# A transformer block on one core: the written order of every engine's steps is set anew, and the inverse lengths get two buffers

## The reference, cut to what matters

```
x  = x + ga * trajectories(layernorm(x) * (1 + ca) + sa)     # "new": guidance mix over an 8-row window
y  = layernorm(x) * (1 + cb) + sb
for layer in (0, 1):
    q, k, v = split(shift_token(y) @ wqkv)                   # "proj": 8 heads of 64
    q, k = rotary(l2norm(q) * qs), rotary(l2norm(k) * ks)    # inverse lengths, then turning
    y = y + local_attention(q, k, v) @ wo                    # "a": windows of 64, each sees itself and the last
    h = layernorm(shift_token(y)) * lg + lb
    y = y + (a * gelu(g)) @ w2 + b2, with a, g = split(h @ w1 + b1)      # "ff"
out = x + gb * y
```

## Time and profile before

| | |
|---|---|
| median of three runs | 968.1 us (965.94 to 968.76) |
| the profiled execution, its own time | 966.96 us |
| its span, first to last instruction | 965.0 us |
| mean granted clock of PE | 0.942 of full |
| busy: PE, DVE, ACT, POOL | 786.4, 668.0, 659.3, 539.6 us |
| chain that ended last | PE 40%, DVE 20%, ACT 19%, "issue" 11%, POOL 9% |

### The profile page before, as it was taken

The page is one execution under the profiler, slowest core; times in us unless marked ns, Lnnn a source line. Parts: engine busy times, 40 slices in busy tenths (PEclk is TensorE's granted clock), DMA queues, the critical chain, the costliest instruction groups (busy, mean ns, idle before and its releaser), DMA issues.

```text
span 965.0 us, 19306 instructions
## 1 busy us (share of the span) xinstructions
PE 786.4 (81%) x7151; PEld 556.3 (58%) x7151; DVE 668.0 (69%) x1588; ACT 659.3 (68%) x1545; POOL 539.6 (56%) x324
## 2 busy tenths in 40 slices
...
DMA packets 12275, 9.85 MB, mean 10 GB/s; under 512 B 1040, under 2 KB 11288, under 8 KB 12184
## 3 DMA queue, kind: packets, MB, share of 16 engines
...
## 4 chain that ended last, share of the span: by engine, by line
PE 40%; DVE 20%; ACT 19%; issue 11%; POOL 9%; DMA 0%; SPq 0%; POOLq 0%; ACTq 0%; DVEq 0%
ACT probs L964 7%; PE pair L696 6%; PE mixed L727 5%; POOL qk L1494 4%; PE dense L831 4%; PE pair L759 3%; DVE space L1393 3%; DVE q_norm L1398 3%; PE dense L795 3%; PE dense L796 2%; PE dense L797 2%; DVE qk L1195 2%; PE dense L908 2%; ACT squares L1083 2%; ACT probs_t L972 2%
## 5 line engine op out<-in xcount | busy, mean ns | idle before, releaser
L1494 POOL TENSOR_TENSOR qk<-space 128x512 f32<-128x512 f32 x128 | 186.4, 1463 | 58.0 <-DVE q_norm L1398 55.1
L1454 POOL TENSOR_TENSOR root<-power,minus_half 128x32 f32<-128x32 f32 x32 | 174.0, 5438 | 4.6 <-DVE power L1404 4.6
L964 ACT ACTIVATE probs<-pair,neg_max 128x128 f32<-128x128 f32 x512 | 138.3, 402 | 18.9 <-DVE neg_max L1215 18.5
L1393 DVE TENSOR_TENSOR space<-dense,tables 128x512 f32<-128x512 f32 x128 | 87.5, 684 | 36.9 <-ACT space L1087 35.2
L908 PE MATMUL dense<-wq_hi,h_hi 128*128 128x512 f32 x192 | 90.2, 470 | 26.6 <-DVE space L1393 10.9
L1491 POOL TENSOR_TENSOR space<-space,tables 128x512 f32<-128x512 f32 x64 | 82.7, 1293 | 50.7 <-ACT space L1087 50.7
L696 PE MATMUL pair<-eye_s,probs 128*128 128x128 f32 x512 | 80.9, 292 | 34.9 <-ACT probs L964 34.7
L1215 DVE TENSOR_REDUCE neg_max<-pair 128x4 f32<-128x512 f32 x128 | 82.0, 684 | 35.2 <-PE pair L759 35.1
L1083 ACT ACTIVATE squares<-dense 128x512 f32<-128x512 f32 x128 | 79.1, 618 | 39.5 <-PE dense L910 38.6
L696 PEld LDWEIGHTS pair<-eye_s,probs 128*128 128x128 f32 x512 | 59.1, 146 | 56.2 <-ACT probs L964 51.9
L1398 DVE TENSOR_REDUCE q_norm<-squares 128x8 f32<-128x512 f32 x128 | 86.4, 675 | 0.0
...
## 6 DMA issues: line engine op xcount, KB each, us to landing
...
```

Source lines behind the costliest of these rows:

```text
L964: last = act.activation(probs[:, ring, hh, :], banks[m][:, hh * P:(hh + 1) * P], ACT.Exp, bias=neg_max[:, ring, hh:hh + 1], scale=1.0)
L1393: dve.tensor_tensor(turned_s[:, t % 2, m, :].rearrange("p (h a b) -> p h a b", h=HEADS, a=2), halves[:, :, ::-1, :], rot(layer, t, 2 * m + 1),
L1454: return pool.tensor_tensor(to, of, minus_half[:, 0:of.shape[-1]], ALU.pow)
L1494: pool.tensor_tensor(qk[s][:, t, m * INNER:(m + 1) * INNER], turned_c[:, t % 2, m, :], turned_s[:, t % 2, m, :], ALU.add).then_inc(added, 1)
```

## The change

Three things change, and no instruction is added or removed apart from waits.

1. `power` and `root` become `powers` and `roots` with two buffers each, used in turn by pair of tiles. `proj.rsqrt` on DVE additionally waits until the root of two pairs ago is written, and the root on POOL until the scaling of two pairs ago has been done.
2. All lists of `ORDER` except the lead-in are rewritten. Of 672 PE steps 338 stand at another place, of 592 on ACT 369, of 544 on DVE 262, of 240 on POOL 64, by at most 14 places.
3. With it the banks `dense`, which are dealt out in PE's order, fall to other steps.

```diff
-        power, root, scratch = sb("power", [P, 32]), sb("root", [P, 32]), sb("scratch", [P, 1])
+        powers, roots, scratch = sb("powers", [P, 2, 32]), sb("roots", [P, 2, 32]), sb("scratch", [P, 1])
...
-                dve.tensor_tensor(rows, rows, root[:, :].rearrange("p (h o) -> p h o", o=1)
+                dve.tensor_tensor(rows, rows, roots[:, pair_ % 2, :].rearrange("p (h o) -> p h o", o=1)
...
-                    dve.tensor_scalar(power[:, :], q_norm[:, :], 1e-24, None, ALU.max).then_inc(qk_powered, 1)
+                    if past(pair_ - 1):
+                        dve.wait_ge(qk_rooted, pair_ - 1)
+                    dve.tensor_scalar(powers[:, pair_ % 2, :], q_norm[:, :], 1e-24, None, ALU.max).then_inc(qk_powered, 1)
...
-                inverse_root(root[:, :], power[:, :]).then_inc(qk_rooted, 1)
+                if past(pair_ - 1):
+                    pool.wait_ge(qk_ready, pair_ - 1)
+                inverse_root(roots[:, pair_ % 2, :], powers[:, pair_ % 2, :]).then_inc(qk_rooted, 1)
```

The moves of which the text below speaks, as they stand in turn 1, unless said otherwise (`...` leaves out steps):

```diff
 PE, slot 1 to 2
-1:a.flip.2 1:proj.tile.1.1 1:proj.tile.1.2 1:a.mix.2 1:proj.tile.2.0 ... 1:a.flip.3 1:a.out.2 1:a.mix.3 1:proj.tile.3.0 1:proj.tile.3.1 1:proj.tile.3.2 1:a.out.3 2:new.dots 1:a.project 2:proj.tile.0.0 2:a.turn.0
+1:a.flip.2 1:proj.tile.1.1 1:proj.tile.1.2 1:proj.tile.2.0 1:a.mix.2 ... 1:proj.tile.3.0 1:a.flip.3 1:proj.tile.3.1 1:a.mix.3 1:proj.tile.3.2 1:a.out.2 2:new.dots 1:a.out.3 1:a.project 2:a.turn.0 2:a.turn.1 2:proj.tile.0.0
 PE, slot 0
-0:a.flip.2 0:proj.tile.0.0 0:proj.tile.0.1 0:proj.tile.0.2 0:a.mix.2 0:proj.tile.1.0 0:proj.tile.1.1 0:proj.tile.1.2 0:a.flip.3 0:proj.tile.2.0 ...
+0:a.flip.2 0:proj.tile.0.0 0:proj.tile.0.1 0:proj.tile.0.2 0:proj.tile.1.0 ... 0:proj.tile.2.2 0:a.flip.3 0:a.mix.2 0:a.mix.3 0:proj.tile.3.0 ...
 DVE, slot 1 to 2
-1:a.mix.2 1:proj.tile.2.0 1:proj.tile.2.1 1:a.mix.3 1:proj.tile.3.0 1:proj.unit.0 1:proj.tile.3.1 2:proj.split 1:proj.rsqrt.1 2:new.dots 1:a.project
+1:proj.tile.2.0 1:proj.tile.2.1 1:a.mix.2 1:proj.tile.3.0 1:proj.tile.3.1 1:a.mix.3 1:proj.rsqrt.1 2:proj.split 1:proj.unit.0 1:a.project
 DVE, slot 1, feed-forward
-1:ff.hi 1:a.mix.0 1:a.unit 1:a.mix.1 1:ff.up.0
+1:ff.hi 1:a.mix.0 1:ff.up.0 1:a.unit 1:ff.up.1 1:a.mix.1
 DVE, slot 1 to 2, turn 3
-1:a.mix.2 1:proj.tile.2.0 1:proj.tile.2.1 1:a.mix.3 1:proj.tile.3.0 1:proj.unit.0 1:proj.tile.3.1 2:proj.split
+1:proj.tile.2.0 1:proj.tile.2.1 1:a.mix.2 1:a.mix.3 1:proj.tile.3.0 1:proj.tile.3.1 2:proj.split 1:proj.unit.0
 DVE, slot 2
-2:new.gate 2:ff.hi 2:new.again
+2:ff.hi 2:new.gate 2:new.again
 POOL, slot 1 (turns 1 to 3)
-1:ff.stats 1:a.rsqrt 2:new.stats 1:ff.hi
+1:ff.stats 1:a.rsqrt 1:ff.hi 2:new.stats
 POOL, slot 1, turn 2
-1:proj.split 2:new.steps 1:proj.tile.0.0 ... 1:proj.rsqrt.0 1:proj.tile.2.0 ... 2:proj.split 1:proj.tile.3.1
+1:proj.split 1:proj.tile.0.0 ... 2:new.steps 1:proj.rsqrt.0 2:proj.split 1:proj.tile.2.0 ... 1:proj.tile.3.1
 ACT, slot 3, turn 2
-3:ff.norm 3:new.sims 3:a.out.2 ... 3:ff.up.0
+3:new.sims 3:a.out.2 3:ff.norm ... 3:ff.up.0
```

More of the change, by code:

```diff
@@ L65 @@
[L65 to L91, removed]
@@ L145 @@
+        2:a.mix.2 2:a.out.2 2:a.flip.3 2:ff.up.2 2:a.mix.3 2:ff.down 2:a.out.3 2:a.project 2:store.turn
+        3:ff.stats 3:ff.norm 3:ff.up.0 3:ff.up.1 3:ff.up.2 3:ff.down 3:store.turn"""),
     ],
@@ L280 @@
-        2:proj.tile.3.0 2:a.mix.3 2:proj.tile.3.1 2:new.gate 2:ff.hi 2:new.again 2:a.project 2:proj.rsqrt.1
-        2:new.stream 2:ff.up.0 2:ff.up.1 2:ff.up.2 3:a.unit 2:ff.down 3:proj.split 3:a.score.0 3:a.score.1
-        2:store.turn 2:proj.keep 3:proj.tile.0.0 3:proj.tile.0.1 3:a.mix.0 3:proj.tile.1.0 3:new.stats
-        3:proj.tile.1.1 3:new.turn 3:proj.rsqrt.0 3:proj.tile.2.0 3:proj.tile.2.1 3:a.mix.1 3:ff.stats
-        3:a.score.2 3:ff.norm 3:a.score.3 3:proj.unit.0 3:new.dots 3:a.mix.2 3:proj.tile.3.0 3:new.sims
@@ L312 @@
[L312 to L316 removed]
+        2:new.stats 2:new.turn 2:proj.split 2:proj.tile.0.0 2:proj.tile.0.1 2:proj.tile.1.0 2:proj.tile.1.1
@@ new lines @@
+        2:new.weights 2:a.mix.1 2:proj.tile.0.0 2:proj.tile.0.1 2:proj.tile.1.0 2:proj.tile.1.1
+        2:proj.rsqrt.0 2:proj.tile.2.0 2:proj.tile.2.1 2:a.score.2 2:a.score.3 2:ff.stats 2:ff.norm
+        2:a.mix.2 2:proj.unit.0 2:proj.tile.3.0 2:a.mix.3 2:proj.tile.3.1 2:ff.hi 2:new.gate 2:new.again
+        2:ff.up.0 2:new.stream 2:proj.rsqrt.1 2:ff.up.1 2:a.project 2:ff.up.2 3:a.unit 3:proj.split
+        2:ff.down 3:a.score.0 3:a.score.1 2:store.turn 2:proj.keep 3:proj.tile.0.0 3:proj.tile.0.1
```

497 lines of the change are left out of this document (262 added, 235 removed).

## The result

The changed kernel takes 982.96 us (median of 4 runs, 981.34 to 984.42) against 967.02 (965.27 to 968.76): ratio 1.0167, 95% interval 1.0149 to 1.0185, 16 us slower. The forecast was 953.0, and its range ended at 974. The profiled execution took 984.01 us, its span was 982.1 and PE's mean granted clock 0.946.

A forecast was written before the change was run, and what follows sets the result against it. No engine bounds the kernel as a whole; PE's 178.6 us of idle time is what an order can win from. Terms 5.7 + 3.6 + 1.5 + 1.3 + 3 = 15.1 us gave 968.1 - 15.1 = 953.0 us, range 935 to 974.

The forecast's parts named there:

- the rest of the order: Hundreds of swapped steps not priced singly, bounded by turn 2's list reaching turn 1's level: 3 us won, bounds 0 and 8.
- What bounds the kernel: No engine as a whole; 58 us stretches between projections are those where POOL is fullest, 41.2 us, the most anywhere.
- Two buffers: Second buffers for power and root: their added waits cost nothing, and by themselves they free nothing.
- `h_lo` ahead of `new.stats`: POOL, slot 1 of three turns: h_lo right behind the long root, 5.7 us won, bounds 0 and 6.0.
- The hand-over: Slot 1 to slot 2: bank for new.dots free earlier, projection at full clock; 3.6 us won, bounds 0 and 7.
- The clock at `ff.up`: PE, 214 to 221: shorter stop may keep the clock, granted 0.52 before; 1.5 us won, bounds 0 and 3.1.
- Table loads: ACT, turn 2: 3:new.sims ahead of 3:ff.norm saves two loads; 1.3 us won, bounds 0 and 2.6.
- Tiles ahead of attention: Rival: PE tiles waiting for banks delay attention, some 3 us in slots 0 and 1 of four turns; 977 us, chance 0.17.
- Nothing: Rival: waits removed come back at the next meeting of attention and POOL; about 968 us, chance 0.11.
- the 3 us priced there: POOL, turn 2: 2:proj.split ahead of 1:proj.tile.2.0 waits for the last product, a loss of some 3 us.
- The lock rule: Rival: long root blocks a DVE scaling, up to 5.4 us in each of three slots 1; 969 us, chance 0.02.

The follow-up runs named there:

- e4: Changed kernel with POOL's new.dots of slot 3 put back behind the additions of proj.tile.2.0 and 2.1, turns 1 and 2: 974.19 us, ratio 1.0083.
- e7: Kernel before with only POOL's new.dots of slot 3 moved ahead of proj.tile.2.0 and 2.1 additions, turns 1 and 2: 977.62 us, ratio 1.0098.
- e11: Kernel before plus two buffers, with only the late steps of 3|0 in the new order on PE, ACT and DVE: 970.14 us, ratio 1.0038.
- e1: Changed code with two buffers and their waits, but every list of the kernel before: 966.95 us, ratio 1.0005.
- e8: Kernel before plus two buffers, with only turn 1's hand-over from slot 1 to 2 in new order on PE, ACT, DVE: 970.41 us, ratio 1.0029.
- e3: Changed kernel with the new order only up to the projection of 1|1 and the order of before after it: 967.03 us, ratio 1.0002.
- e6: e4 with POOL's turn 2 list partly put back (new.steps ahead of slot 1's additions, proj.split behind tile 3.0's): 980.60 us, ratio 1.0126.
- e13: Kernel before plus two buffers, with the edits of e7 and e11 together: 979.24 us, ratio 1.0121.
- e5: e4 with the late steps of 3|0 also in the old order on PE, ACT and DVE: 974.10 us, ratio 1.0067.

## Why the prediction was wrong

The step that failed is "the rest of the order": "I take 3", with the bounds 0 and 8. It compared lengths of stretches and let a rewritten order only gain. POOL's list was short enough to read to the end (64 moved steps), but `new.dots` of slot 3 is in no term. That the two would meet could have been seen in the trace of before: POOL did the three operations of tile 2 from 342.3 to 346.2 and waited for `new.dots` until 348.5, with `new.sims` right behind; in the new order the three start there. In place of 3 us won, that move alone lost some 8 (e4) to 11 (e7), and the late steps of 3|0, in no term either, another 3 (e11).

*What bounds the kernel.* POOL's 41.2 us were not the most anywhere: 634 to 692 has 41.8, and the stretch 412 to 470 has 43.97. That the long stretches are the fullest of POOL holds all the same.

*Two buffers*: nothing, as said (e1).

*`h_lo` ahead of `new.stats`*, 5.7: the mechanism was right and the size off. POOL did what was written to 0.1 us, but "nothing else hides these, for PE waits there" was wrong: PE's row of `ff.up` in 1|1, which the prediction did not read, shows a wait of 0.73 us for `h_lo`, since `a.out.0` ahead of it was late too. 2.9 us by the medians, of which the trace shows 1.3.

*The hand-over*, 3.6: the stop of `new.dots` went (3.48 to 0.81 us) and the projection came when forecast, but still 5.29 us long. "With no such stop it runs at full clock" was the wrong step: the clock was 0.83 in 249 to 259 with waits of 0.81 and 0.69 us only. The term counted the shorter projection as won by the order. Alone the hand-over cost 2.8 us (e8).

*The clock at `ff.up`*, 1.5: the stretch of 0.52 went to 1.00, and the stretch up to 1|1 fell by 4.8 us, all of it clock by the table (6.6 to 1.7). That the stretch came out near the forecast is luck, then: at full clock it is 53.8 us before and 53.9 after, so neither `h_lo` nor the hand-over shows in it. What was won there came back as other stretches of half clock, 4.9 us in the bracket of 1|3 alone. Over all stretches from 1|0 to 4|2 the brackets add up to 18.4 us before and 16.6 after, so in sum the clock does not explain the 16 us.

*Table loads*, 1.3: two fewer, and nothing won. In e4 the stretch up to 2|3 is 61.1 us at full clock; before it is 62.9 less 1.9.

*The rivals.* "Tiles ahead of attention" named a true mechanism and put it wrong: not 3 us in each of eight slots, but 3.7 in one (3|0, e11), at most 1.2 in 2|0, and nothing in the length of 1|0 (47.8 us against 48.2, though at full clock that would be 47.8 against 46.3). Its 977 us were the nearest number, for a reason that is shown for a quarter of the loss. "Nothing" was right for e3, where the lead did not last. 2|1 and 2|2 together grew by 1.8 us, near the 3 us priced there; that POOL's queue did it is not shown (e6). The lock rule struck elsewhere than at the root: in neither trace does a scaling start inside a long root, so that case stays untested, and the small operations of `new.sims` that do take 0.15 to 0.18 us there.

*Open.* 11.7 of the 16 us are shown by adding (e13). In e5, with both undone, about 7 remain, spread over 1|2, 1|3, 2|0, the hand-over of turn 2, the join before 3|0 and the clock; no run isolates them. The tiles may be part of it. PE's waits over the whole run, before and then after:

```profile
PE dense L908 <- DVE space L1393: 10.9, 20, 1.0
PE dense L908 <- ACT v L1093: 1.9, 2, 0.9
PE pair L696 <- ACT probs L964: 34.7, 54, 4.7
PE pair L696 <- DVE o_rows L1227: 4.2, 6, 1.7
```
```profile
PE dense L909 <- DVE space L1394: 23.4, 28, 1.9
PE dense L909 <- ACT v L1094: 9.9, 11, 1.6
PE pair L697 <- ACT probs L965: 19.5, 43, 2.1
PE pair L697 <- DVE o_rows L1228: 17.9, 17, 3.5
```

The columns are us in total, times and the longest. Tiles wait for their banks 20.5 us longer, and the transposes behind DVE's division 13.7 us longer; for the exponentials PE waits 15.2 us less. In e5 the first two rows still have 25.0 and 7.3 us. So the new order trades one wait for another all along, which is what that rival describes, and how much of the open part it makes is not shown.

Why the same order gets the half clock in one trace and not in another (e3, e5) is open too.
